# Delta stage: the keys' squares in one transfer, norms and substitution a slot sooner, half of the output sums on ScalarE

## The reference, cut to what matters

```python
q = _short_conv_silu(h @ Wq, conv_q_w); k = ...; v = ...
q = _l2norm(q) * scale; k = _l2norm(k)
beta = sigmoid(h @ Wb); g = -exp(A_log) * softplus(h @ Wa + dt_bias)
def step(S, inp):
    S = S * exp(g_t)
    delta = (v_t - k_t @ S) * b_t
    S = S + outer(k_t, delta)
    return S, q_t @ S
o = _rmsnorm(o, onorm_w) * silu(h @ Wg)
x = x + o @ Wo
```

## Time and profile before

| | us |
|---|---|
| median of 3 runs | 3739.05 (3738.07 to 3743.66) |
| profiled execution, its own time | 3734.4 |
| its span in the trace | 3731.8 |
| TensorE busy | 3259.0 (87%) |
| VectorE busy | 2696.1 (72%) |
| ScalarE busy | 2039.6 (55%) |
| GpSimd busy | 1799.9 (48%) |

### The profile page before, as it was taken

The page is one execution under the profiler, slowest core; times in us unless marked ns, Lnnn a source line. Parts: engine busy times, 40 slices in busy tenths (PEclk is TensorE's granted clock), DMA queues, the critical chain, the costliest instruction groups (busy, mean ns, idle before and its releaser), DMA issues. The chain is left out here.

```text
span 3731.8 us, 87201 instructions
## 1 busy us (share of the span) xinstructions
PE 3259.0 (87%) x32714; PEld 2433.8 (65%) x32714; DVE 2696.1 (72%) x5753; ACT 2039.6 (55%) x4599; POOL 1799.9 (48%) x1631
## 2 busy tenths in 40 slices
PE   4789999999999999788998999977987699899998
PEld 3677777777777777655666566654665466656665
DVE  5577777777777777477777677776998577767775
ACT  3466666666666666315665466623443466536662
POOL 3355555555555555235664366621222566436662
PEclk9699999999999999999999999997999899999999
DMA  4111111111111110042122212231121222221122
GB/s 125 23 25 27 26 27 26 26 26 27 37 28 25 27 28 13 14 134 52 45 68 68 63 47 53 60 94 45 47 59 44 64 53 67 56 75 47 45 72 71
DMA packets 409630, 182.71 MB, mean 49 GB/s; under 512 B 235808, under 2 KB 384384, under 8 KB 406656
## 3 DMA queue, kind: packets, MB, share of 16 engines
q1 hardware_dynamic: 409216, 177.15, 19.4%
HBM read 94.47 MB, written 40.12 MB: 36 GB/s over the span
## 5 line engine op out<-in xcount | busy, mean ns | idle before, releaser
L1206 POOL TENSOR_TENSOR delta_cv<-delta_cv,delta_last_tap 96x256 f32<-96x256 f32 (+1 forms) x384 | 332.7, 866 | 615.1 <-DVE delta_cv L1639 614.2
L1947 POOL TENSOR_TENSOR g_a_rn<-g_a_clip,g_minus_half 128x16 f32<-128x16 f32 x64 | 186.4, 2912 | 271.1 <-DVE g_a_clip L2211 242.8
L1947 POOL TENSOR_TENSOR f_a_rn<-f_a_clip,f_minus_half 128x16 f32<-128x16 f32 x64 | 186.3, 2911 | 260.5 <-DVE f_a_clip L2211 232.2
L2164 ACT ACTIVATE g_a_pr<-g_ps,g_a_nb,g_a_rn 128x128 f32<-128x128 f32 x512 | 185.9, 468 | 146.8 <-DVE g_a_nb L2245 146.8
L2164 ACT ACTIVATE f_a_pr<-f_ps,f_a_nb,f_a_rn 128x128 f32<-128x128 f32 x512 | 185.9, 468 | 146.3 <-DVE f_a_nb L2245 146.3
L1631 DVE SCALAR_TENSOR_TENSOR delta_cv<-delta_ps,delta_conv_qk,delta_cv 96x256 f32<-96x256 f32 x256 | 122.2, 477 | 189.0 <-ACT delta_last_tap L1474 186.9
L1472 ACT ACTIVATE delta_cv<-delta_ps,delta_conv_qk 96x256 f32<-96x256 f32 x256 | 121.3, 474 | 236.6 <-PE delta_ps L1303 235.7
L1247 PE MATMUL delta_ps<-delta_state,delta_qk 96*128 96x192 f32 x1024 | 200.5, 340 | 23.2 <-issue 18.8
L1247 PEld LDWEIGHTS delta_ps<-delta_state,delta_qk 96*128 96x128 f32 x1024 | 169.5, 194 | 37.4 <-issue 33.9
L1631 DVE SCALAR_TENSOR_TENSOR delta_cv<-delta_ps,delta_conv_v,delta_cv 128x256 f32<-128x256 f32 x192 | 92.1, 480 | 109.1 <-ACT delta_last_tap L1474 107.5
L1472 ACT ACTIVATE delta_cv<-delta_ps,delta_conv_v 128x256 f32<-128x256 f32 x192 | 90.7, 472 | 135.8 <-PE delta_ps L1303 135.7
(11 more groups left out here) (350 smaller groups left out, 10350.7 us busy)
## 6 DMA issues: line engine op xcount, KB each, us to landing
f_a_vm<-f_a_v SPq DMA_DIRECT2D x128, 130.0 KB, 2.3
g_a_vm<-g_a_v SPq DMA_DIRECT2D x128, 130.0 KB, 2.3
delta_gd<-delta_dram_row SPq DMA_DIRECT2D x16, 1024.0 KB, 4.7
window_vm<-window_v SPq DMA_DIRECT2D x64, 128.0 KB, 2.3
f_m_x<-y SPq DMA_DIRECT2D x24, 256.0 KB, 3.5
delta_dram_inv<-delta_sub SPq DMA_DIRECT2D x16, 256.0 KB, 2.1
f_m_more<-x SPq DMA_DIRECT2D x16, 256.0 KB, 3.9
x<-f_m_x SPq DMA_DIRECT2D x16, 256.0 KB, 2.3
```

The lines of the kernel that those rows point to most:

```text
L1206: pool.tensor_tensor(cv[0:M, t % 3], cv[0:M, t % 3], last_tap[0:M, t % 3], ALU.add).then_inc(summed.sem, 1)
L1947: pool.tensor_tensor(rn[:, u % 2], clip[:, u % 2], minus_half[:], ALU.pow).then_inc(rn_sb.sem, 1)
L2164: e = act.activation(pr[:, u % 2, half, i, :], ps[:, score_bank(u, half), i * P:(i + 1) * P], ACT.Exp, bias=nb[:, u % 2, half, i:i + 1], s ...
```

## The change

The keys' squares come back in one transfer: `diag_d` gets rows of 272 elements for each block, so that the diagonal elements of all blocks lie a constant 17 apart. Norms, rates and substitution are written a slot sooner (14, 14, 15 to 18), and with them the four tiles that VectorE finishes alone (now 15 to 18). For even chunks ScalarE's Square gives the sums itself, head by head, and VectorE's reduce runs for odd chunks only. Scores of the second half of the heads, one gate matmul, the gated multiplies, the odd chunk's transposes and its y change slots.

```diff
-    diag_d = nc.dram_tensor(name + "_dram_diag", (B16, 2, H, 16, 16), F32).ap()
+    diag_d = nc.dram_tensor(name + "_dram_diag", (2, H, B16, 16 * 17), F32).ap()
-    K_NORM = 15
-    SOLVE_AT = 16
-    KK_AT, KQ_AT = ((6, 7), (9, 10)), ((13, 14), (17, 18))
+    K_NORM = 14
+    SOLVE_AT = 15
+    KK_AT, KQ_AT = ((6, 7), (9, 10)), ((13, 14), (18, 19))
-    GATE_AT, OT_AT, Y_AT = ((2, 2, 5), (2, 5, 12)), ((21, 22, 25), (21, 22, 25)), (27, 27)
+    GATE_AT, OT_AT, Y_AT = ((2, 5, 6), (2, 5, 12)), ((21, 22, 25), (19, 20, 23)), (27, 25)
...
-                        sp.dma_start(diag_d[b].rearrange("c h j i -> j c h i"), al1[r, :, :, r]).then_inc(diag_out.sem, 16)
+                        sp.dma_start(diag_d[:, :, b, 0:256].rearrange("c h (j i) -> j c h i", i=16), al1[r, :, :, r]).then_inc(diag_out.sem, 16)
...
-                    for b in range(B16):
-                        squares = diag_d[b].rearrange("c h j i -> (j i) (c h)")[0:256:17, :]
-                        sp.dma_start(n2k[16 * b:16 * b + 16, :], squares, allow_slow_non_contiguous=True).then_inc(n2k_in.sem, 16)
+                    squares = diag_d.rearrange("c h b (j s) -> (b j) s (c h)", s=17)[:, 0, :]
+                    sp.dma_start(n2k[:], squares, allow_slow_non_contiguous=True).then_inc(n2k_in.sem, 16)
...
-                    C = chunk(t, 14 + i)
+                    C = chunk(t, 13 + i)
                     if C is not None:
                         osq_sb.need(pool, C)
                         copied(pool, ("gate", C, 2))
...
-                    C = chunk(t, 16 + i)
+                    C = chunk(t, 15 + i)
                     if C is not None:
                         of_sb.need(pool, C)
...
-                    act.activation(vr[:, C % 3, mine], o[:, C % 2, mine], ACT.Square).then_inc(osq_sb.sem, 1)
+                    if C % 2 == 0:
+                        of_sb.need(act, C - 1)
+                        for h in heads(i):
+                            e = act.activation(vr[:, C % 3, h, :], o[:, 0, h, :], ACT.Square, accum_out=ostat[:, 0, h:h + 1])
+                    else:
+                        e = act.activation(vr[:, C % 3, mine], o[:, 1, mine], ACT.Square)
+                    e.then_inc(osq_sb.sem, 1)
...
-                    C = chunk(t, 11 + i)
+                    C = chunk_of(t, 11 + i, 1)
                     if C is not None:
                         osq_sb.need(dve, C, i + 1)
                         mine = slice(HB * i, HB * i + HB)
-                        dve.tensor_reduce(ostat[:, 0, mine], vr[:, C % 3, mine], AX.X, ALU.add).then_inc(ostat_step.sem, 1)
+                        dve.tensor_reduce(ostat[:, 0, mine], vr[:, C % 3, mine], AX.X, ALU.add).then_inc(osum_sb.sem, 1)
```

More of the change, by code:

```diff
@@ L908, in delta_attention @@
     diag_in = mark("diag_in", 16)
-    n2k_in = mark("n2k_in", 16 * B16)
+    n2k_in = mark("n2k_in", 16)
     beta_in = mark("beta_in", 16)
@@ L953, in delta_attention @@
     osq_sb = mark("osq_sb", 2)
-    ostat_step = mark("ostat_step", 3)
+    osum_sb = mark("osum_sb", 2)
+    ostat_sb = mark("ostat_sb")
     of_sb = mark("of_sb")
@@ L1134, in _ @@
                     inv_out.need(sp, n - 1)
-                    sp.dma_start(sub[:, 0], diag_d.rearrange("b c h j i -> (b c h) j i")).then_inc(diag_in.sem, 16)
+                    sp.dma_start(sub[:, 0].rearrange("p j i -> p (j i)"), diag_d[:, :, :, 0:256].rearrange("c h b e -> b (c h) e")).then_inc(diag_in.sem, 16)
                     betas = row_d[1, 2 * H * n:2 * H * (n + 1), :].rearrange("r (b i) -> b r i", i=16)
@@ L1235, in _ @@
                 if C is not None:
-                    ostat_step.need(pool, C)
+                    ostat_sb.need(pool, C)
                     o_normed.need(pool, C - 1)
@@ L1515, in misc @@
                             bvr_sb.need(act, n)
-                            ostat_step.need(act, C - 3, 2)
+                            if (C - 3) % 2 == 0:
+                                osq_sb.need(act, C - 3)
+                            else:
+                                osum_sb.need(act, (C - 3) // 2)
                             bank = take(act, ("vt", n, cc, m))
@@ L1606, in output_norm @@
                     q_summed.need(dve, C)
-                    ostat_step.need(dve, C - 2)
+                    ostat_sb.need(dve, C - 2)
                     dve.tensor_scalar(q_eps[:, C % 2], q_sum[:, C % 2], 1e-6 * DK, 1e-12 * DK, ALU.mult, ALU.add)\
@@ L1618, in output_norm @@
                     of_sb.need(dve, C - 1)
-                    ostat_step.need(dve, C, 2)
+                    if C % 2 == 0:
+                        osq_sb.need(dve, C)
+                    else:
+                        osum_sb.need(dve, C // 2)
                     q_eps_sb.need(dve, C)
                     dve.scalar_tensor_tensor(out=ostat[:, 1, :], in0=ostat[:, 0, :], scalar=1.0 / DV, in1=q_eps[:, C % 2],
-                                             op0=ALU.mult, op1=ALU.add).then_inc(ostat_step.sem, 1)
+                                             op0=ALU.mult, op1=ALU.add).then_inc(ostat_sb.sem, 1)
             def taps(t):
```

## The result

The changed kernel takes **3712.76 us** (median of four runs, 3703.74 to 3716.16) where the kernel before took 3738.56 beside it: a ratio of 0.9928, with a 95% interval of 0.9912 to 0.9943, or 25.8 us less. That is faster by more than 0.2%, 7.8 us above the forecast of 3705 and inside its range. The profiled execution is the fastest of the four: 3703.74 us, with a span of 3702.0.

What follows compares the result with a forecast made beforehand. TensorE's order was nearly full, its waits set by VectorE's chain to kd and GpSimd's to the gate. GpSimd's chain limited the gain to 2.1 us a unit, 16 times, 34 us: 3739 - 34 = 3705 us, range 3680 to 3727.

Steps and rivals of the forecast that it cites:

- part 1: Norms and rates a slot sooner: 2.5 us earlier on VectorE, GpSimd's chain starts 3.2 us sooner, output sum 1.7 us later.
- part 2: Keys' squares in one transfer: lands in 3.1 us, 1.2 us before norms need it; eight would land 0.9 us late.
- The rival of a slow transfer: The one transfer lands late and stops VectorE, TensorE and GpSimd's chain: 3766 us midway, 3867 at the upper end; chance 0.06.
- part 3: Even chunk's sums on ScalarE: two reduces leave VectorE, slot 20's matmul 2.5 us sooner; ScalarE takes 2.0 us a half.
- The nameless wait: TensorE's wait without a named releaser before L1247 at slot 20, 1.64 us, was to fall under 1 us.
- the upper end: ScalarE's four Squares a half without overlap, each followed by a short instruction: 2.6 us, +1.8 a half.
- part 4: GpSimd's order: its chain keeps 20.8 us and ends 3.2 us sooner; gate and x4 move by 2.1 us.
- The rival that won more: GpSimd's tail doesn't hold the gate, add of tile 21 and its Silu hide: 3.5 us a unit, 3683 us; chance 0.15.
- The rival of the output sum: TensorE doesn't regain 1.7 us behind the output sum, ScalarE adds 1.0: 1.3 us a unit won, 3718 us; chance 0.22.
- parts 4 and 5: Gated multiplies a slot sooner leave the sum alone; moved scores and odd chunk's output win 0.3 us at slot 12, left out.
- The sum: TensorE could reach x4 at 669.1, GpSimd's chain allows 671.0: 2.1 us a unit, 16 times, 34 us.
- the two chains: VectorE's chain to kd sets TensorE's wait at slot 20; GpSimd's, from norms to the gate, sets x4's at slot 23.

Runs made afterwards that it cites:

- e3: The changed kernel with the keys' squares in eight transfers as before: 3715.97 us, ratio 0.9938.
- e4: The changed kernel with VectorE also finishing tiles 20 and 21, GpSimd's adds there: 3671.41 us, ratio 0.9816.
- e6: The changed kernel with scores, gate matmul, transposes, y and gated multiplies back in their old slots: 3760.49 us, ratio 1.0056.
- second run: The changed kernel measured and profiled once more, nothing altered, beside e8, e9 and e10: 3714.79 us, ratio 0.9927.
- e2: The kernel before with only the even chunks' sums on ScalarE (wider rows stay, eight transfers): 3755.82 us, ratio 1.0056.
- e5: The kernel before with only squares in one transfer and norms and substitution a slot sooner: 3773.17 us, ratio 1.0084.
- e8: The changed kernel with four useless matmuls of 252 columns before slot 23's values' transposes: 3689.57 us, ratio 0.9867.
- e1: The changed kernel with ScalarE's sums undone, Square in one piece and VectorE's reduces for all chunks: 3720.18 us, ratio 0.9945.
- e10: The kernel before with VectorE also finishing tiles 21 and 22 (wider rows stay, eight transfers): 3710.56 us, ratio 0.9916.
- e12: e4 with the even chunk's sums back on VectorE: 3712.88 us, ratio 0.9929.
- e9: e2 with the four useless matmuls of e8 added: 3721.48 us, ratio 0.9947.
- e11: The kernel before with only four useless matmuls before slot 23's transposes (wider rows stay): 3728.52 us, ratio 0.9970.

## Why the prediction was right, and where it was not

**Norms and rates (part 1): right.** They stand where they were put, last 633.07 - 631.46 = 1.6 us (predicted 1.7), and the output sum behind them makes TensorE wait 1.57 us (predicted 1.5 to 2).

**The transfer (part 2): right in size, less needed than was said.** It lands in 3.1 us, the estimate; VectorE waits for it once in the run, 3.8 us in the first unit. But e3 shows that eight would have cost a us a unit at most, and nothing that the whole time shows. The rival of a slow transfer fell with the landing.

**ScalarE's sums (part 3): the place right, the term a little too dear.** A half takes 1.48 us where 2.0 were taken: each Square is followed by a read of the accumulator of 0.19 us, but the pair recurs every 0.34 us, so it overlaps. From the first half's kd matmuls to the matmul of slot 20 it is 13.75 us in place of 16.26: 2.5 us sooner, as predicted. The nameless wait is 0.65 us, under the 1 us that was set. The Trainium skill's rule on VectorE's accumulator output ("VectorE: DVE Perf Modes", two Vector instructions with no wait between them) holds on ScalarE too, by the count of rows: two for each. The prediction took that as a reason for the upper end; the rows came out below the middle.

**GpSimd's chain (part 4): right**, at 20.7 us for 20.8, ending 2.95 us sooner for 3.2, and so is what stands behind it, the add of tile 21 and its Silu. One detail is other than told: the instruction that waits is the values' transpose of slot 23, behind that Silu, and the gate is just in time after it. From the first half's kd matmuls to x4 the gain is 1.96 us for 2.1. The rival that won more falls with e4: GpSimd's tail does hold TensorE, for 1.5 us a unit. The rival of the output sum falls with the 2.18 us that TensorE still waits in slot 23: it was early.

**The slots (parts 4 and 5): wrongly costed at nothing.** The prediction said that the gated multiplies' slot "leaves the sum alone" and left part 5 out. By e6 the sum rests on these slots: without them x4 comes 0.4 us sooner in place of 1.96, since `bm` moves with norms and GpSimd idles between its adds, and half clock makes the kernel slower than before. Of a step that moves, the prediction followed the norms, the rates and the adds, and not the instruction whose slot is counted from theirs.

**The sum: 0.4 us a unit too high, with a term missing.** It took 2.1 us a unit sixteen times, 34. Measured: 1.96, less 0.2 given back in the rest of the unit, is 1.7 in units with the full clock. The prediction took the rest of the unit as unchanged. The 14 middle units won 1257.5 - 1237.1 = 20.4 us, the first one 9.6 in the profiled execution and 3.8 in the one of the second run. The missing term is TensorE's clock. In the middle units its half-clock time is the same before and after, 48 us, but not in the same places (eight of ten falls behind the wait of 2.18 us; before, two of nine behind the waits of the earlier trace rows), and nothing in the sum made it so: 102, 140 or 92 us in e2, e6 and e5, 10 in e8. The prediction had set a unit of 87.0 us, and 88 or more as a sign of being wrong. Units with the full clock, as its own rows had it (1.00), take 87.2 us; but the mean of the 14 is 88.4 (89.8 before), past that sign. The change came out near the sum because it happened to leave that time as it was. The sign fits the two chains, which e1, e4, e10 and e12 tested; the size rests in part on luck.

## What to carry to other kernels

Follow each chain to the instruction on which it meets TensorE's order, and look for every instruction whose place is counted from the one you move: one of 1.05 us that slips in front of the last link eats half of the gain. Where TensorE is nearly full, don't add up its waits alone; look at where they lie and at the clock behind them, since taking one wait away can move and lengthen another so that the clock falls behind it, and that can cost more than the wait did (e2). Count the falls by place before and after, and not their sum alone. The next step here is e4, which moves two adds off the busiest tail and beats both kernels by 1.1% and 1.8%; e4 with e8's filling matmuls was not tried.

## What the runs showed of the hardware

- TensorE's clock falls to half for 3.4 to 10.2 us in the middle of a stage in which TensorE is busy for nine tenths; matmuls of 192 columns then take 2.93 us for eight in place of 1.57.
- Such a fall stood behind a pause of 2.18 us in eight of 14 units (the changed kernel; seven in its second profile), behind pauses of up to 1.89 and 1.49 us close together in ten of 14 (e2), behind one of 1.49 in one of 14 (before), and at none of these places once the pause was filled (e8, e9). Other falls, three to eight in 14 units, stood 12 to 14 us into a unit with no pause over 1.1 us near them (before, e2, e9, e10, e11); what brings them is open.
- Some 7 us at half clock made a unit 2.7 to 3.8 us longer in the changed kernel, and hardly longer in e10, where a wait behind the fall took up the delay.
- Four useless matmuls of 252 columns a unit, 1.97 us in a wait of 2.18, made the program 25 us faster, and 34 us in e2; in the kernel before it was 11, with more half clock in the middle units and not less.
- A Square of 192 columns with an accumulator output is 0.35 us on ScalarE, with 0.19 us for the read, and the next one starts 0.09 us after the read does: one pair every 0.34 us.
- One transfer of 2048 elements of four bytes lands in 3.1 us, while each of eight with 256 took 1.8.
